# Second product of a mixture-of-experts layer: w2 held in the array and tokens streamed, results turned back a tile later, eight tile sizes in place of six

## The chip, the core and the metric

One core of a Trainium2 chip runs the whole program in one launch. The metric is the time of one execution in microseconds (us). TensorE (PE) multiplies; a matrix product is issued as pairs of a weight load (PEld) of up to 128x128 and a product that streams a second operand past it, one column at a time. VectorE is DVE, ScalarE is ACT, GpSimd is POOL and SyncE, which here only starts transfers, is SP.

## The reference, cut to what matters

2048 tokens of 256 numbers pass a fixed mixing step (each token is rotated by quaternions and scaled by a gate), a router picks one of 8 experts for each, and the expert's gated two-layer network is added to the input:

```
h = x_rot @ w1[e] + b1[e];  a, g = split(h)          # 256 -> 2 x 1024
y = (a * sigmoid(g)) @ w2[e] + b2[e]                  # 1024 -> 256
out = x + y      # e is the expert with the largest router logit of the token
```

All data are float32. With the inputs that are drawn, the experts get 308, 336, 181, 195, 258, 268, 327 and 175 tokens.

## The kernel before, in words

**Early part** (to about 36 us). x is loaded and turned, the rotation matrices are built, the router's logits and the place of every token in its expert's list are worked out on chip, the rotated rows are written to a table in memory (`x_rows`), and a small table (`ctrl`) gets one word per tile with its size class and expert. Near its end PE runs products on zeros (`keep_warm`, `keep_warm_long`).

**Tiles.** There is one tile for each expert, tile 0 to tile 7, of up to 512 tokens in four subtiles of 128; more tiles are taken only if an expert has over 512 tokens, which does not happen here. POOL gathers the rows of a tile by indirect transfers, one for each subtile (`gather`, into `xg`), gathers the rows of x to which the result is added (`fetch`, into `y_out`), and scatters finished rows (`scatter`), always for four subtiles. Its order in tile i is: wait until PE has turned the rows of tile i, gather(i+1), wait for the result of tile i-1, scatter(i-1), fetch(i+1). SP loads the next expert's weights as soon as the raw copies are split.

**Precision.** Every product of two float32 matrices is made of three products of a fast format (fp32r): hi by hi, hi by lo, lo by hi. ACT copies the high part of w1, w2, the tile's rows and u, DVE subtracts it for the low part. All `_hi` and `_lo` names are these.

**First product** (`first_product`, lines 1082 to 1108). w1 is held, the tile's tokens stream. For each of 8 chunks c of hidden units and for g and a, 6 products of n columns follow each other: 96 products for a tile. n is not the number of tokens but the least entry of `SIZES` that holds it; PE has one copy of the body for each size and picks it by comparisons (`by_size`). DVE, ACT and POOL only know the number of subtiles, 2, 3 or 4, and work on 256, 384 or 512 columns (line 602 and line 891 and on). While PE works on chunk c, ACT takes the sigmoid of g (L573), DVE multiplies (L821), ACT and DVE make u_hi (L579) and u_lo (L827).

**Turning the next rows** (`turn_held`, L1057). After the first product of tile i, PE turns the gathered rows of tile i+1, two transposes for each subtile in use.

**Second product** (`second_product`, `row_blocks`, lines 1110 to 1137). Here u is held, 128 tokens at a time, and w2 streams, 256 columns wide: 8 chunks x 3 products for each subtile in use. y comes out with tokens on the partitions, ready to be added to the rows. Subtiles 3 and 2 come first where there are any, then 1, then 0.

**After it.** DVE adds b2, spread over all partitions in `b2_all`, to the fetched rows at chunk 6 of the first product (L836), and adds y to them at chunk 2 of the next tile's first product, in two instructions, one for each bank of y (L850); the scatters of subtiles 0 and 3 go when the first is done, those of 1 and 2 when the second is. For the last tile `add_last` (L858, L863) adds subtile 1 after its products, while those of subtile 0 still run, and each is scattered when it is added (`end_blocks`).

**Code of PE.** `visit` and `landing` are a jump to a place in the later code and back, made in the early part; the landings stand behind the bodies of five of the six sizes.

## Time and profile before

| | |
|---|---|
| median of 3 runs | 214.83 us (214.12 to 215.44) |
| the profiled execution: first to last instruction | 213.9 us |
| the profiled execution's own time as a run | not given beside its span |
| tiles 0 to 7, from the first product of tile 0 to the last of tile 7 | 36.3 to 209.5 us |
| busy: PE, DVE, POOL, ACT | 95%, 74%, 60%, 57% |
| moved by DMA | 41.26 MB, 193 GB/s |

The profile is of one execution. Busy time of PE counts each product from its start until its result is out, so that neighbours overlap: the distance from start to start says how fast the engine works, the duration of one does not. The three runs listed have no span beside them; the 0.9 us between the median and the profiled span is taken as what lies around the span.

### The profile page before, as it was taken

How to read it: one execution, taken by the hardware profiler on the slowest of the kernel's cores; microseconds unless marked ns; L12 is line 12 of the kernel's file. 1: busy time of each engine (PE TensorE's matmuls, PEld its weight loads, DVE VectorE, ACT ScalarE, POOL GpSimd, SP SyncE). 2: the span in 40 equal slices, each digit the busy share in tenths (PEclk: the TensorE clock that was granted, in tenths of full speed). 3: DMA queues.
4: the chain of work that ended last, by engine and by line, in shares of the span. 5: the costliest groups of instructions: out<-in, count | busy, mean ns of one | idle time of the engine just before them, and what ended most of it. 6: DMA issues, size and time to landing. Idle time of an engine off the chain costs nothing.

```text
span 213.9 us, 4367 instructions
## 1 busy us (share of the span) xinstructions
PE 202.7 (95%) x1512; PEld 191.0 (89%) x1513; DVE 158.0 (74%) x308; ACT 122.5 (57%) x206; POOL 129.2 (60%) x163
## 2 busy tenths in 40 slices
PE   7997779999999999999998999999999999999991
PEld 3877625999999999999998999899999999999991
DVE  4918936789928996598888969993998479874950
ACT  2454861576727482667585767564949185735620
POOL 6002467876802888287878877885487817820751
PEclk9999969999999999999999999999999999999998
DMA  5993744889775174937499479738535691820011
GB/s 144 393 365 122 291 142 116 265 300 311 215 193 227 63 259 97 361 90 264 103 296 317 131 219 320 259 76 292 223 135 168 204 287 69 256 44 0 25 40 37
DMA packets 17540, 41.26 MB, mean 193 GB/s; under 512 B 2920, under 2 KB 11241, under 8 KB 15338
## 3 DMA queue, kind: packets, MB, share of 16 engines
q1 hardware_dynamic: 12784, 30.48, 39.9%
q0 software_dynamic: 4512, 10.50, 19.4%
q14 instruction: 19, 0.16, 0.2%
q8 instruction: 7, 0.11, 0.2%
q10 hardware_dynamic: 218, 0.01, 0.1%
HBM read 36.78 MB, written 6.03 MB: 200 GB/s over the span
## 4 chain that ended last, share of the span: by engine, by line
PE 57%; POOL 13%; DVE 12%; issue 7%; DMA 7%; ACT 2%; DVEq 0%; POOLq 0%; ACTq 0%
PE y_ps L1121 7%; DMA xg<-x_rows,g_idx 7%; PE y_ps L1122 6%; PE y_ps L1123 6%; POOL y_out L429 5%; PE g_ps L1101 5%; POOL out_dram L438 5%; PE g_ps L1106 5%; PE g_ps L1102 4%; PE a_ps L1106 4%; PE a_ps L1102 4%; PE a_ps L1101 4%; PE y_ps L931 3%; POOL xg L417 3%; DVE arena L821 3%
## 5 line engine op out<-in xcount | busy, mean ns | idle before, releaser
L438 POOL DMA_INDIRECT out_dram<-y_out,s_idx x30 | 42.1, 1403 | 41.5 <-DVE y_out L850 30.8
L573 ACT ACTIVATE arena<-g_ps,b_t 128x384 f32<-128x384 f32 (+1 forms) x64 | 34.5, 538 | 47.4 <-PE g_ps L1106 47.4
L821 DVE SCALAR_TENSOR_TENSOR arena<-a_ps,b_t,arena 128x384 f32<-128x384 f32 (+1 forms) x64 | 36.1, 564 | 30.5 <-PE a_ps L1106 27.6
L1121 PE MATMUL y_ps<-w_hi,u_hi 128*128 128x256 f32 x168 | 48.6, 289 | 0.1
L429 POOL DMA_INDIRECT y_out<-in_x_dram,g_idx x32 | 42.4, 1325 | 9.8 <-issue 9.8
L1122 PE MATMUL y_ps<-w_lo,u_hi 128*128 128x256 f32 x168 | 47.5, 283 | 0.0
L1123 PE MATMUL y_ps<-w_hi,u_lo 128*128 128x256 f32 x168 | 47.5, 283 | 0.0
L417 POOL DMA_INDIRECT xg<-x_rows,g_idx x32 | 37.2, 1164 | 13.7 <-issue 9.1
L712 DVE TENSOR_TENSOR w_lo<-w_raw,w_hi 128x1024 fp32r<-128x1024 f32 x32 | 37.2, 1220 | 4.8 <-DMA xg<-x_rows,g_idx 3.6
L579 ACT ACTIVATE u_hi<-arena 128x384 fp32r<-128x384 f32 (+1 forms) x64 | 30.7, 479 | 15.5 <-DVE arena L821 15.5
L1101 PE MATMUL g_ps<-xr_hi,w_hi 128*128 128x256 f32 (+3 forms) x128 | 36.9, 301 | 0.3 <-issue 0.2
L1102 PE MATMUL g_ps<-xr_hi,w_lo 128*128 128x256 f32 (+3 forms) x128 | 36.6, 299 | 0.0
L1101 PE MATMUL a_ps<-xr_hi,w_hi 128*128 128x256 f32 (+3 forms) x128 | 36.6, 299 | 0.0
L1102 PE MATMUL a_ps<-xr_hi,w_lo 128*128 128x256 f32 (+3 forms) x128 | 36.6, 299 | 0.0
L1121 PEld LDWEIGHTS y_ps<-w_hi,u_hi 128*128 128x128 f32 x168 | 32.2, 192 | 0.9 <-DVE u_lo L827 0.5
L827 DVE TENSOR_TENSOR u_lo<-arena,u_hi 128x384 fp32r<-128x384 f32 (+1 forms) x64 | 32.0, 500 | 1.1 <-ACT u_hi L579 0.3
L1122 PEld LDWEIGHTS y_ps<-w_lo,u_hi 128*128 128x128 f32 x168 | 32.2, 192 | 0.0
L1123 PEld LDWEIGHTS y_ps<-w_hi,u_lo 128*128 128x128 f32 x168 | 32.2, 192 | 0.0
L526 ACT ACTIVATE w_hi<-w_raw 128x1024 fp32r<-128x1024 f32 x32 | 31.2, 1058 | 0.0
L1106 PE MATMUL g_ps<-xr_lo,w_hi 128*128 128x256 f32 (+3 forms) x128 | 28.1, 300 | 0.0
L1106 PE MATMUL a_ps<-xr_lo,w_hi 128*128 128x256 f32 (+3 forms) x128 | 27.9, 299 | 0.0
L1101 PEld LDWEIGHTS g_ps<-xr_hi,w_hi 128*128 128x128 f32 x128 | 24.2, 189 | 1.0 <-issue 0.8
(167 smaller groups left out, 297.0 us busy)
## 6 DMA issues: line engine op xcount, KB each, us to landing
w_raw<-in_L_ffn_w_dram SPq DMA_DIRECT2D x16, 1024.0 KB, 8.5
w_raw<-in_L_ffn_w_dram SPq DMA_DIRECT2D x16, 512.0 KB, 5.0
arena<-in_x_dram SPq DMA_DIRECT2D x4, 512.0 KB, 5.9
x_rows<-arena SPq DMA_DIRECT2D x8, 256.0 KB, 2.6
b_all<-in_L_ffn_b_dram SPq DMA_DIRECT2D x1, 1024.0 KB, 5.1
xg<-x_rows,g_idx POOLq DMA_INDIRECT x32, 6.1
y_out<-in_x_dram,g_idx POOLq DMA_INDIRECT x32, 4.2
out_dram<-y_out,s_idx POOLq DMA_INDIRECT x30, 4.0
```

The costliest lines, as they stand in the source:

```text
L417: nc.gpsimd.indirect_dma_start(out=xg[:, s * DIM:(s + 1) * DIM], out_offset=None, in_=x_rows, in_offset=bass.IndirectOffsetOnAxis(ap=g_idx ...
L429: nc.gpsimd.indirect_dma_start(out=y_out[i % YB][:, s * DIM:(s + 1) * DIM], out_offset=None, in_=x_flat, in_offset=bass.IndirectOffsetOnAx ...
L438: nc.gpsimd.indirect_dma_start(out=out_flat, out_offset=bass.IndirectOffsetOnAxis(ap=s_idx[:, i * NSUB + s:i * NSUB + s + 1], axis=0), in_ ...
L573: nc.scalar.activation(sig[:, c % SIG_RING, 0:n], pair[c % RING][1][:, 0:n], ACT.Sigmoid, bias=b1_t[:, bass.ds(e * (2 * NC) + (NC + c), 1) ...
L712: V.tensor_tensor(unit_of(w1_lo, u), raw_unit(u), unit_of(w1_hi[:, :].bitcast(F32), u), ALU.subtract)\
L821: V.scalar_tensor_tensor(u32[:, c % (8 - SIG_RING), 0:n], pair[c % RING][0][:, 0:n], b1_t[:, bass.ds(e * (2 * NC) + c, 1)], sig[:, c % SIG ...
L1101: T.matmul(dst, w_part(w1_hi, k), xh, start=(k == 0), stop=False)
L1102: T.matmul(dst, w_part(w1_lo, k), xh, start=False, stop=False)
L1106: last = T.matmul(dst, w_part(w1_hi, k), xr_lo[:, k * ITEM:k * ITEM + n], start=False, stop=(k == KH - 1))
L1121: T.matmul(dst, u_hi[:, uv], w2_hi[:, wv], start=first, stop=False)
L1122: T.matmul(dst, u_hi[:, uv], w2_lo[:, wv], start=False, stop=False)
L1123: last = T.matmul(dst, u_lo[:, uv], w2_hi[:, wv], start=False, stop=final)
```

## The change

The second product holds w2 and streams the tokens. For each half h of the 256 outputs and each chunk c there are 3 products of n columns, where n is the tile's size class; y comes out with the outputs on the partitions (`y_half[h]`). ACT adds b2 there as a bias, one number for each partition, while it copies y to `yt` in SBUF (`biased`, 336 columns whatever the tile; the first half's copy stands between the second and the third part of the next w1 split, the second half's behind the fourth). PE turns `yt` back with six transposes at chunk 2 of the next tile's first product (`turn_back_rows`), into the banks from which it came, and DVE adds the result to the rows in one instruction. A fourth subtile, where a tile has one, is turned ahead of the first product. The last tile is followed by its two copies, eight transposes, and an addition and a scatter for each subtile in use.

`SIZES` goes from six entries to eight, with 224 as the least; the tiles of this input have the classes 320, 336, 224, 224, 272, 272, 336, 224, where they had 320, 352, 256, 256, 288, 288, 352, 256. DVE and ACT work on 256 columns for two subtiles and 336 for three, where it was 384. The load of b2 to all partitions (1 MB) goes; b2 comes as 16 rows early, and is turned on PE with b1. PE has a copy of the second product for each size. Landings stand behind all eight sizes, with three more visits in the early part.

```diff
-    SIZES = (256, 288, 320, 352, 384, 512)
+    SIZES = (224, 256, 272, 288, 304, 320, 336, 512)
     BLOCKS = [(size + P - 1) // P for size in SIZES]
+    WIDTH = {blocks: max(size for size, b in zip(SIZES, BLOCKS) if b == blocks) for blocks in BLOCKS}
+    TURNED = 3
...
-    LANDINGS = (0, 1, 2, 3, 5)
+    LANDINGS = tuple(range(len(SIZES)))
...
+        b_t = sb("b_t", P + KH * NE)
+        b1_t = b_t[:, 0:P]
+        b2_t = b_t[:, P:P + KH * NE]
+        yt = sb("yt", KH * ITEM)
...
-        y_ps = [ps(f"y{h}_ps") for h in range(2)]
+        y_ps = ps("y_ps", KH * 512)
+        y_half = [y_ps[:, h * 512:(h + 1) * 512] for h in range(KH)]
...
@@ -303,6 +309,7 @@
             for g in range(4):
                 sp.dma_start(x_tok[:, 4 * g:4 * g + 4, :], xv[:, 4 * g:4 * g + 4, :]).then_inc(x_loaded[g], 16)
             sp.dma_start(b1_rows[:, :], b1.rearrange("e (c f) -> (e c) f", f=P)).then_inc(b1_loaded, 16)
+            sp.dma_start(b2_rows[:, :], b2.rearrange("e (h f) -> (e h) f", f=P)).then_inc(b2_loaded, 16)
...
             load_w2(0, 1)
-            for s in range(NSUB):
-                sp.wait_ge(gathered[s], 16)
-            sp.dma_start(b2_all[:, :], b2.rearrange("e d -> (e d)").partition_broadcast(P)).then_inc(b2_loaded, 16)
             for e in range(1, NE):
...
+            nc.gpsimd.memset(yt[:, :], 0.0).then_inc(yt_set, 1)
...
             def scatter(i):
-                for s in (0, 3, 1, 2):
-                    if PLACE[s] == 0:
-                        pool.wait_ge(y_done[BANK[s]], i + 2)
+                pool.wait_ge(y_done, i + 2)
+                for s in range(NSUB):
                     scatter_block(i, s)
...
             def end_blocks(blocks):
 
-                pool.wait_ge(last_added, 1)
-                for s in range(1, min(blocks, 3)):
+                for s in range(blocks):
+                    pool.wait_ge(last_added, s + 1)
                     scatter_block(NE - 1, s)
-                pool.wait_ge(last_added, 2)
-                scatter_block(NE - 1, 0)
-                if blocks == NSUB:
-                    pool.wait_ge(last_added, 3)
-                    scatter_block(NE - 1, 3)
...
                 if i > 0:
-                    act.wait_ge(mm2_done, i)
+                    act.wait_ge(half_done[KH - 1], i)
...
             act.wait_ge(b1_turned, 1)
-            nc.scalar.activation(b1_t[:, :], early_ps[:, 0:P], ACT.Copy).then_inc(b1_t_done, 1)
+            nc.scalar.activation(b_t[:, :], early_ps[:, 0:P + KH * NE], ACT.Copy).then_inc(b1_t_done, 1)
...
+            def biased(i, e, h, first, cols, done=None):
+                act.wait_ge(half_done[h], i + 1)
+                put = nc.scalar.activation(yt[:, h * ITEM + first:h * ITEM + cols], y_half[h][:, first:cols], ACT.Identity,
+                                           bias=b2_t[:, bass.ds(e * KH + h, 1)])
+                if done is not None:
+                    put.then_inc(done, 1)
...
                 if 0 < i < NE:
                     for u in range(W1U):
                         w1_hi_part(i, u)
+                        if u % 2 == 1:
+                            biased(i - 1, i - 1, u // 2, 0, FIRST, yt_done[u // 2])
...
+                biased_rest(i, e, n)
+                if i >= NE - 1:
+                    for h in range(KH):
+                        biased(i, e, h, 0, FIRST, yt_done[h])
...
-                if_blocks(act, this_word(act, word_at), lambda blocks: gate_tile(e, e, blocks * P))
+                if_blocks(act, this_word(act, word_at), lambda blocks: gate_tile(e, e, WIDTH[blocks]))
...
+            def add_rows(i):
                 dve.wait_ge(x_fetched[i % YB], (i // YB + 1) * NSUB * 16)
-                rows = y_out[i % YB][:, 0:blocks * DIM].rearrange("p (s d) -> p s d", s=blocks)
-                V.tensor_tensor(rows, rows, b2_all[:, bass.ds(e * DIM, DIM)].unsqueeze(1).to_broadcast([P, blocks, DIM]),
-                                ALU.add).then_inc(b2_added, 1)
...
-            def add_rows(i):
-                dve.wait_ge(mm2_done, i + 1)
-                dve.wait_ge(b2_added, i + 1)
-                for h in range(2):
-                    half = bank_rows(i, h)
-                    V.tensor_tensor(half, y_ps[h][:, :].rearrange("p (s d) -> p s d", s=2), half, ALU.add)\
-                        .then_inc(y_done[h], 1)
+                dve.wait_ge(y_turned, i + 1)
+                rows, y = rows_of(i, 0, NSUB)
+                V.tensor_tensor(rows, y, rows, ALU.add).then_inc(y_done, 1)
...
             def add_last(i, blocks):
 
-                dve.wait_ge(b2_added, i + 1)
-                dve.wait_ge(outer_done, i + 1)
-                rows = bank_rows(i, 1)[:, 0:min(blocks - 1, 2)]
-                V.tensor_tensor(rows, y_ps[1][:, :].rearrange("p (s d) -> p s d", s=2)[:, 0:min(blocks - 1, 2)], rows,
-                                ALU.add).then_inc(last_added, 1)
-                dve.wait_ge(mm2_done, i + 1)
-                for a in range(2 if blocks == NSUB else 1):
-                    rows = bank_rows(i, 0)[:, a]
-                    V.tensor_tensor(rows, y_ps[0][:, a * DIM:(a + 1) * DIM], rows, ALU.add).then_inc(last_added, 1)
-                dve.wait_ge(last_added, 3 if blocks == NSUB else 2)
-                for h in range(2):
-                    dve.sem_inc(y_done[h], 1)
+                dve.wait_ge(x_fetched[i % YB], (i // YB + 1) * NSUB * 16)
+                dve.wait_ge(y_turned, i + 1)
+                for s in range(blocks):
+                    rows, y = rows_of(i, s, 1)
+                    V.tensor_tensor(rows[:, 0], y[:, 0], rows[:, 0], ALU.add).then_inc(last_added, 1)
+                dve.wait_ge(last_added, blocks)
+                dve.sem_inc(y_done, 1)
...
-                n = blocks * P
+                n = WIDTH[blocks]
...
-                    if c == 6:
-                        add_b2(i, e, blocks)
                 lo_u(i, NC - 1, n)
...
                 if f == 3:
                     visit(2)
+                if f == 6:
+                    visit(7)
...
                 rotate_blocks(b)
+                if b == 3:
+                    visit(8)
                 if b == 5:
                     visit(4)
+                if b == 6:
+                    visit(9)
             pe.wait_ge(b1_loaded, 16)
-            T.transpose(early_ps[:, 0:P], b1_rows[:, :], ident[:, :]).then_inc(b1_turned, 1)
+            pe.wait_ge(b2_loaded, 16)
+            T.transpose(early_ps[:, 0:P], b1_rows[:, :], ident[:, :])
+            T.matmul(early_ps[:, P:P + KH * NE], b2_rows[:, :], ident[0:KH * NE, 0:KH * NE], start=True, stop=True)\
+                .then_inc(b1_turned, 1)
 
...
+            def turn_back(subs):
+                for h in range(KH):
+                    for s in subs:
+                        last = T.transpose(y_half[h][:, s * P:(s + 1) * P], yt[:, h * ITEM + s * P:h * ITEM + (s + 1) * P],
+                                           ident[:, :])
+                return last
+            def turn_back_rows(at1, blocks):
+                for h in range(KH):
+                    pe.wait_ge(yt_done[h], at1)
...
+            def first_product(size, i, at1):
                 n = SIZES[size]
                 for c in range(NC):
+                    if c == 2:
+                        with pe.If(((i - 1) & 15) < NE - 1):
+                            turn_back_rows(at1, TURNED)
...
-            def row_blocks(subs, at1, done=None):
-                for c in range(NC):
-                    pe.wait_ge(u_lo_done[c], at1)
-                    wv = slice(c * DIM, (c + 1) * DIM)
-                    for s in subs:
-                        at = c * ITEM + s * P
-                        uv = slice(at, at + P)
-                        dst = y_ps[BANK[s]][:, PLACE[s] * DIM:(PLACE[s] + 1) * DIM]
-                        first = c == 0 and s == subs[0]
-                        final = c == NC - 1 and s == subs[-1]
-                        T.matmul(dst, u_hi[:, uv], w2_hi[:, wv], start=first, stop=False)
-                        T.matmul(dst, u_hi[:, uv], w2_lo[:, wv], start=False, stop=False)
-                        last = T.matmul(dst, u_lo[:, uv], w2_hi[:, wv], start=False, stop=final)
-                if done is not None:
-                    last.then_inc(done, 1)
...
+            def second_product(size, at1):
+                n = SIZES[size]
                 pe.wait_ge(w2_split, at1)
-                for h in range(2):
-                    pe.wait_ge(y_done[h], at1)
-                with pe.If(f_size(word) >= BLOCKS.index(4)):
-                    row_blocks((3,), at1)
-                with pe.If(f_size(word) >= BLOCKS.index(3)):
-                    row_blocks((2,), at1)
-                row_blocks((1,), at1, done=outer_done)
-                row_blocks((0,), at1, done=mm2_done)
+                pe.wait_ge(y_done, at1)
+                for h in range(KH):
+                    dst = y_half[h][:, 0:n]
+                    for c in range(NC):
+                        if h == 0:
+                            pe.wait_ge(u_lo_done[c], at1)
+                        wv = slice(c * DIM + h * P, c * DIM + (h + 1) * P)
+                        uv = slice(c * ITEM, c * ITEM + n)
+                        T.matmul(dst, w2_hi[:, wv], u_hi[:, uv], start=(c == 0), stop=False)
+                        T.matmul(dst, w2_lo[:, wv], u_hi[:, uv], start=False, stop=False)
+                        last = T.matmul(dst, w2_hi[:, wv], u_lo[:, uv], start=False, stop=(c == NC - 1))
+                    last.then_inc(half_done[h], 1)
...
+            def first_and_landing(size, i, at1):
+                first_product(size, i, at1)
+                if size in LANDINGS:
+                    landing(LANDINGS.index(size) + 2)
...
                     at1 = pe.to_reg(i + 1)
+                    next1 = pe.to_reg(i + 2)
                     at16 = pe.to_reg(i * 16 + 16)
                     next16 = pe.to_reg(i * 16 + 32)
...
-                    by_size(word, 0, len(SIZES) - 1, lambda size: first_product(size, at1))
+                    with pe.If(pe.snap(size_before, min_val=0, max_val=len(SIZES) - 1) >= BLOCKS.index(NSUB)):
+                        turn_back_rest(at1)
+                    by_size(word, 0, len(SIZES) - 1, lambda size: first_and_landing(size, i, at1))
+                    pe.reg_mov(size_before, 0)
                     with pe.If(i < NE - 1):
+                        pe.reg_mov(size_before, f_size(word))
                         after = pe.snap(next_word, min_val=0, max_val=127)
                         pe.wait_ge(pair_free[NC - RING], at1)
                         turn_held(after, next16)
-                    second_product(word, at1)
+                    by_size(word, 0, len(SIZES) - 1, lambda size: second_product(size, at1))
+                    with pe.If(i >= NE - 1):
+                        turn_back_rows(next1, NSUB)
+                    pe.nop()
```

## Rows read from the trace of the kernel before

**Rows 1.** The page, busy time, share of the span and instructions; this is PE.

```profile
PE 202.7 (95%) x1512; PEld 191.0 (89%) x1513; DVE 158.0 (74%) x308; ACT 122.5 (57%) x206; POOL 129.2 (60%) x163
```

**Rows 2.** Windows: all tiles, then tiles 2 to 5; length, busy per engine, clock, DMA.

```profile
36.27:209.55 173.28, 172.12 (x1309) 169.83 (x1308) 135.17 (x205) 105.30 (x179) 113.98 (x87) 1.00 0.60 190
84.69:102.88 18.19, 18.19 (x151) 17.78 (x150) 13.86 (x25) 12.50 (x23) 12.11 (x9) 1.00 0.68 225
102.88:122.04 19.16, 18.34 (x153) 18.11 (x152) 16.46 (x28) 12.71 (x23) 15.50 (x13) 1.00 0.75 230
122.04:144.91 22.87, 22.64 (x174) 22.11 (x174) 19.50 (x28) 14.42 (x23) 18.30 (x16) 1.00 0.66 204
144.91:167.56 22.65, 22.54 (x175) 22.02 (x175) 18.32 (x26) 14.42 (x23) 15.62 (x13) 1.00 0.57 198
```

**Rows 3.** Windows: the second products of tiles 1, 4 and 5.

```profile
75.97:84.69 8.72, 8.72 (x75) 8.72 (x74) 7.10 (x10) 4.86 (x7) 7.26 (x5) 1.00 0.54 160
...
135.50:144.91 9.41, 9.23 (x75) 8.92 (x74) 8.39 (x11) 5.60 (x8) 7.58 (x7) 1.00 0.54 169
158.39:167.56 9.17, 9.11 (x76) 8.82 (x74) 8.38 (x11) 5.59 (x8) 7.34 (x7) 1.00 0.59 186
```

**Rows 4.** Timeline of PE, tiles 3 and 4: first and last of 16 such pairs.

```profile
103.36 0.40 PE L1106 MATMUL g_ps<-xr_lo,w_hi 128*128 128x256 f32 x2
...
114.16 0.40 PE L1106 MATMUL a_ps<-xr_lo,w_hi 128*128 128x256 f32 x2
...
122.56 0.42 PE L1106 MATMUL g_ps<-xr_lo,w_hi 128*128 128x288 f32 x2
...
134.41 0.43 PE L1106 MATMUL a_ps<-xr_lo,w_hi 128*128 128x288 f32 x2
```

**Rows 5.** Chain of waits, tile 6, n = 352: first and last of 16 such pairs.

```profile
168.44 0.32 PE g_ps L1106 x2
...
182.83 0.32 PE a_ps L1106 x2
```

**Rows 6.** Timeline of PE, early part: plain float32 products, 128 columns (`rotate_blocks`).

```profile
19.54 1.06 PE L1002 MATMUL g_ps<-b_all,x_t 128*128 128x128 f32 x8
...
22.22 1.06 PE L1002 MATMUL a_ps<-b_all,x_t 128*128 128x128 f32 x8
```

**Rows 7.** Chain of waits, the turning before tile 4: a gather, one transpose.

```profile
108.46 6.65 DMA xg<-x_rows,g_idx
...
115.59 0.11 PE a_ps L1057
```

**Rows 8.** Waits of PE for tile 4's rows: total, times, longest us.

```profile
PE a_ps L1057 <- DMA xg<-x_rows,g_idx: 0.6, 1, 0.6
```

**Rows 9.** Timeline of DVE and POOL in tile 2: both additions, first scatter.

```profile
89.97 1.28 DVE L850 TENSOR_TENSOR y_out<-y_ps,y_out 128x512 f32<-128x512 f32 x2
...
90.93 1.02 POOL L438 DMA_INDIRECT out_dram<-y_out,s_idx  x1 [3.88 <-DVE y_out L850]
```

**Rows 10.** Timeline of the end: last product, last addition, last scatter.

```profile
209.30 0.28 PE L1123 MATMUL y_ps<-w_hi,u_lo 128*128 128x256 f32 x1
209.61 0.42 DVE L863 TENSOR_TENSOR y_out<-y_ps,y_out 128x256 f32<-128x256 f32 x1 [2.38 <-PE y_ps L1123]
210.31 0.98 POOL L438 DMA_INDIRECT out_dram<-y_out,s_idx  x1 [1.82 <-DVE y_out L863]
```

**Rows 11.** The page, costliest groups: ACT's sigmoids and the idle time before them.

```profile
L573 ACT ACTIVATE arena<-g_ps,b_t 128x384 f32<-128x384 f32 (+1 forms) x64 | 34.5, 538 | 47.4 <-PE g_ps L1106 47.4
```

**Rows 12.** Waits, all engines: POOL in the early part.

```profile
POOL over L398 <- DVE sm L749: 15.4, 1, 15.4
```

**Rows 13.** Timeline of DVE, tile 1: the addition of b2, between products.

```profile
75.21 0.95 DVE L836 TENSOR_TENSOR y_out<-y_out,b_all 128x768 f32<-128x768 f32 x1
```

**Rows 14.** Chain of waits, just ahead of the loop over the tiles.

```profile
31.14 1.07 issue
```

**Rows 15.** The page, DMA queues: packets, MB, share of 16 engines.

```profile
q8 instruction: 7, 0.11, 0.2%
```

More of the change, by code:

```diff
@@ L118, in early @@
             taken[0] += cols
-            return b2_all[0:rows, taken[0] - cols:taken[0]]
+            return scratch[0:rows, taken[0] - cols:taken[0]]
         q_rows = sb("q_rows", QD, rows=13)
         b1_rows = early(P, P)
+        b2_rows = early(KH * NE, P)
         sgn_l = early(P, 64)
@@ L244, in adaln_moe_ffn_kernel @@
         u_lo_done = [sem(f"u_lo_done{c}") for c in range(NC)]
-        mm2_done = sem("mm2_done")
-        outer_done = sem("outer_done")
+        half_done = [sem(f"half_done{h}") for h in range(KH)]
+        yt_set = sem("yt_set")
+        yt_done = [sem(f"yt_done{h}") for h in range(KH)]
+        y_turned = sem("y_turned")
         last_added = sem("last_added")
-        y_done = [sem(f"y_done{h}") for h in range(2)]
+        y_done = sem("y_done")
         scattered = [sem(f"scattered{b}") for b in range(YB)]
@@ L580, in hi_u, with biased_rest @@
                     .then_inc(u_hi_done, 1)
+            FIRST = WIDTH[NSUB - 1]
+            def biased(i, e, h, first, cols, done=None):
[4 more added lines that the diff above has]
+                    put.then_inc(done, 1)
+            def biased_rest(i, e, n):
+                if n > FIRST:
+                    for h in range(KH):
+                        biased(i, e, h, FIRST, n)
             def gate_tile(i, e, n):
@@ L828, in lo_u, with rows_of @@
                                 u_hi[:, at:at + n].bitcast(F32), ALU.subtract).then_inc(u_lo_done[c], 1)
-            def add_b2(i, e, blocks):
-                if i == 0:
-                    dve.wait_ge(b2_loaded, 16)
+            def rows_of(i, first, count):
+                return (y_out[i % YB][:, first * DIM:(first + count) * DIM].rearrange("p (s h d) -> p s h d", s=count, h=KH),
+                        y_ps[:, :].rearrange("p (h s d) -> p s h d", h=KH, s=NSUB)[:, first:first + count])
@@ L1080, in turn_first, with turn_back_rest @@
                         keep_warm(late_ps, 3)
-            def first_product(size, at1):
+            def turn_back(subs):
[5 more added lines that the diff above has]
+            def turn_back_rows(at1, blocks):
+                for h in range(KH):
+                    pe.wait_ge(yt_done[h], at1)
+                turn_back(range(blocks)).then_inc(y_turned, 1)
+            def turn_back_rest(at1):
+                for h in range(KH):
+                    pe.wait_ge(yt_done[h], at1)
+                turn_back(range(TURNED, NSUB))
+            def first_product(size, i, at1):
                 n = SIZES[size]
                 for c in range(NC):
+                    if c == 2:
+                        with pe.If(((i - 1) & 15) < NE - 1):
+                            turn_back_rows(at1, TURNED)
                     if c % CPU1 == 0:
@@ L1142, in by_size @@
                     body(low)
-                    if low in LANDINGS:
-                        landing(LANDINGS.index(low) + 2)
                     return
```

24 lines of the change are left out of this document (10 added, 14 removed).

## The prediction

> **What bounds the kernel now.** I read the busy times first: PE is busy for 95% of the span, nobody else above 74% [rows 1]. That alone would also be true of an engine that waits often and briefly, so the next view is the timeline, where only distances between starts count. In tile 3, at n = 256, there are 90 products from the first start shown to the last, in 10.80 us: 0.1200 us each. In tile 4, n = 288, it is 11.85/90 = 0.1317 [rows 4]; in tile 6, n = 352, 14.39/90 = 0.1599 [rows 5]. These are dense, and the cost follows the columns. The windows then give what is not dense: tile 3 takes 19.16 us where tile 2, of the same size, takes 18.19 [rows 2], partly for two more transposes and 0.6 us because PE waits for the gathered rows of tile 4 [rows 8]; and a second product of 72 streams, which should take 72 x 0.12 = 8.64 us and takes 8.72 in tile 1, takes 9.41 and 9.17 in tiles 4 and 5 [rows 3], where DVE is late with u_lo. So PE bounds all eight tiles, POOL's gathers touch the path once, and 173.28 us [rows 2] is the part that can move. The granted clock is 1.00 in it, the 2.4 GHz level.
>
> **The second product.** Before, 24 products of 256 columns for each subtile in use, 504 in all. After, 48 products of n columns for each tile, 384 in all. n = 272 lies halfway between two rows: 0.1258. For 320 and 336 I go along the line from 288 to 352, 0.00044 us a column: 0.1458 and 0.1529 [rows 4, 5].
> - Tile 0: 8.64 - 48 x 0.1458 = 1.64 us less.
> - Tiles 1 and 6: 8.64 - 48 x 0.1529 = 1.30 less each.
> - Tiles 4 and 5: 9.41 and 9.17 [rows 3] against 48 x 0.1258 = 6.04: 3.37 and 3.13 less. This counts the late u_lo as gone: DVE loses the addition of b2, 0.95 us at the very end of the first product [rows 13], and works on 336 columns where it had 384, and the first pass now takes 3 x 0.126 = 0.38 us for a chunk where it took 0.36, so each u_lo is asked for a little later. Next late would be the sigmoids behind the w2 split on ACT.
>
> **The narrow tiles.** Tiles 2, 3 and 7 go to 224 columns, in 96 + 48 products each. No row shows the fast format below 256. The lines through 256 give 0.1067 (from 352) or 0.1083 (from 288); not a bit faster than now would be 0.1200; a plain float32 product streams 128 columns each 2.68/24 = 0.1117 with the same size of weight load [rows 6], so that a weight load can follow at least that fast. I take 0.110, near that row: 144 x 0.010 = 1.44 us less in each tile, 4.32 in all.
>
> **The first products of the others.** 352 to 336 saves 96 x 0.0070 = 0.67 in tiles 1 and 6, 288 to 272 saves 96 x 0.0059 = 0.57 in tiles 4 and 5, tile 0 keeps 320.
>
> With the 0.6 us wait taken out for now, less work on PE is 1.64 + 2.60 + 6.50 + 4.32 + 1.34 + 1.14 + 0.60 = 18.1 us. Here a page can be weighed against the rows. The Trainium skill, "TensorE: Matmul & The Clock Gate", section "Back-to-back issue gap", puts a warm product at its columns over 2.4 plus 2.5 ns, 0.109 us for 256; the row has 0.1200. By it the second product would fall from 504 x 0.109 = 55.0 to 45.1 us, 9.9 less, where my terms for dense streams give 10.9: the rows make each product that goes dearer, and I go by them.
>
> **Added on PE.** Six transposes in each of tiles 1 to 7, 0.11 us each [rows 7]: 4.62 us, all on the path. PE waits there for ACT's copy of y; ACT starts it as the second product ends, and PE has two chunks (24 products, 2.6 us at least) before it asks, so nothing is late. Left: 18.1 - 4.6 = 13.5 us.
>
> **Moved past other queues.** ACT gets two copies, about 0.54 us each, the mean of its sigmoids [rows 11]; it sat idle 47.4 us in all waiting for PE's g, so they are free; the third and fourth w1 splits wait for the first half of y, about 3 us into the second product, when the first two splits are hardly over, and chunk 4 needs them some 6 us later. If that cover went, ACT's 2 x 0.54 a tile would reach PE's first chunk. Behind the copy of the second half stands the first sigmoid of the tile, whose g comes 0.7 us after. On POOL the memset of `yt` lies within the 15.4 us in which it waits for the counts [rows 12]. On SP one more small load stands ahead of the first weights, and 1 MB of broadcast b2 goes; neither is waited for. The added transpose of b2 and three visits of the early part I cost at nothing, between -0.1 (less DMA) and +1.07 us, the one gap there in which PE waits for nothing shown [rows 14].
>
> **What is late next: the gathers.** POOL's scatter of tile 1 starts 6.24 us after tile 2's first product (90.93 and 84.69 [rows 9, 2]). Now y is added after 0.66 us of transposes, 36 products come 0.36 earlier, and no scatter leaves before both halves are added, half of 1.28 us later [rows 9]: 7.2 us after. Tile 2 starts 1.64 + 1.97 - 0.66 = 2.95 us earlier, at 81.7; the scatter at 88.9. From there POOL has no break until the third gather of tile 4, 17.5 us later (108.46 - 90.93), at 106.4, and this lands 6.65 us after, at 113.1 [rows 7, 9]. PE, which was ready for it at 114.5, is ready 2.95 + (1.44 - 0.66) + (0.96 - 0.66) = 4.0 us earlier, at 110.5. It waits 2.6 us. The same reckoning for tile 5 leaves nothing. Left: 10.9 us.
>
> **The end.** From the start of the last product to the end it is 213.9 - 209.3 = 4.6 us, of which the last 3.6 begin with the last scatter [rows 10]; subtile 1 had gone before. After: 0.31 until y can be read, 0.54 ACT's copy, 0.15 handed on (an estimate, half of the 0.28 from DVE to POOL), 7 x 0.11 to the last transpose's start, 0.31, addition 0.42, 0.28, first scatter and gap 1.28, then 3.6: 7.7 us. 3.1 more, bounds 2 and 4. Net 10.9 - 3.1 = 7.8 us: the span goes from 213.9 to 206.1, and with the 0.9 by which the median of 214.83 stands above the span, **207.0 us**.
>
> **Rivals.**
> - POOL's chain stretches: the 6.65 us of a landing grow, or the scatters run at the slow pace that they have beside DVE's work, and the later tiles wait as well. For: POOL works without a break there, and a shorter tile gives it no less to do. Against: tiles 6 and 7 have slack. The same 2.3 us once more gives 209.3. Chance 0.12.
> - PE's code. It has eight copies of the first product for six, and eight of the second for none. The page shows 7 fetches of instructions on one queue, 0.11 MB [rows 15], and a gap of 1.07 us where the loop's first code is entered [rows 14]. If each of 14 entries (8 second products, and 6 first products of another size than the one before, the first counted) cost 1.07 us, it is 15 us: 222; hidden by a third, half or more, 207 to 217. It decides at 7.8/14 = 0.56 us an entry. Against: PE's stream shows no gap at any tile's start now. Chance 0.15. The Trainium skill, "Runtime: NRT & Kernel Launch", section "Instruction fetch mechanics", speaks for this rival: PE's instruction memory is 128 KiB, filled in 16 KiB blocks, and a branch out of what is held waits for a fetch; no row shows the limit.
> - Slower, by one mechanism: below 256 columns the fast format falls to the plain one's rate. Plain float32 takes two of the shown records for a product (four products in the code stand as x8 [rows 6]), 0.223 us for 128 columns, so 0.39 for 224. 432 narrow products x 0.28 = 121 us: 328. It decides as soon as a narrow product takes 7.8/432 = 0.018 us more than I say, at 0.128. For: nothing in this trace streams it narrower. Against: the cost from 352 to 256 is straight. Chance 0.08.
> - That the size classes do not fit can be excluded: the counts of tokens fix them, and the old classes follow from the same counts.
>
> **Numbers.** The forecast has 0.60, the rivals 0.12, 0.15 and 0.08, and 0.05 is left for what I have not seen. Low end: no wait for gathers (-2.6) and 224 at 0.1067 (-1.4), 203. High end: 224 at 0.1200 (+4.3, of which 0.9 lies in the wait), the gathers' rival (+2.3) give 212.7, and a third of the code's 15 us gives 212; 213.5. What stays out is most of the last rival and the worse half of the code's. A measurement here tells about 1% from no change, so faster is below 212.7 and slower above 217.0. Faster: 0.59 + 0.11 + 0.07 + 0.02 = 0.79. Within: 0.09. Slower: 0.12, 0.08 of it the narrow products.
>
> **What would show it.** L1101 to L1106 at 224 columns about 0.11 us apart, and the second product's 48 streams of tile 4 in some 6.1 us without a gap; one wait of 2 to 3 us of PE's turning ahead of tile 4 and none after; six transposes at chunk 2 that wait for nothing; 7 to 8 us from the last product to the end, with ACT's copy, the eight transposes and two scatters in a row. I am wrong if PE shows gaps at the starts of second products that no engine released (code), if narrow products are over 0.12 apart, or if the tiles 5 to 7 wait for gathers.

## The result: 424.1 us in place of 214.8

The changed kernel takes 424.1 us (median of 4 runs, 419.98 to 440.47, the highest of them in a slower state of the chip), 1.965 times the time of before (95% interval 1.9504 to 1.9795). The forecast of 207.0 us, range 203.0 to 213.5, is wrong by a factor of two, and no rival's time reached it either (the highest was 328).

### The profile page after: what moved, and what is told of

Its sections match the earlier page's. It is cut to its first block, busy times and chain, and to the rows that moved or that the text cites. A ratio compares the mean times of both kernels' runs of the same rounds, so it can differ in the third digit from the quotient of the medians.

```text
span 423.3 us, 4317 instructions
## 1 busy us (share of the span) xinstructions
PE 235.5 (56%) x1444; PEld 218.1 (52%) x1445; DVE 148.0 (35%) x293; ACT 127.8 (30%) x222; POOL 120.7 (29%) x166
## 3 DMA queue, kind: packets, MB, share of 16 engines
q8 instruction: 99, 1.62, 1.9%
## 4 chain that ended last, share of the span: by engine, by line
PE 55%; issue 42%; ACT 1%; DVE 1%; POOL 0%; DVEq 0%
PE y_ps L1158 6%; PE y_ps L1159 5%; PE g_ps L1137 5%; PE y_ps L1160 5%; PE a_ps L1138 5%; PE g_ps L1138 5%; PE g_ps L1142 4%; PE a_ps L1137 4%; PE a_ps L1142 4%; PE y_ps L935 2%; PE y_ps L1099 2%; PE a_ps L1008 1%; PE y_ps L930 1%; PE g_ps L1008 1%; PE a_ps L1070 1%
## 5 line engine op out<-in xcount | busy, mean ns | idle before, releaser
L1137 PE MATMUL g_ps<-xr_hi,w_hi 128*128 128x224 f32 (+3 forms) x128 | 41.2, 335 | 106.6 <-issue 106.6
L844 DVE SCALAR_TENSOR_TENSOR arena<-a_ps,b_t,arena 128x336 f32<-128x336 f32 (+1 forms) x64 | 34.1, 533 | 157.4 <-PE a_ps L1142 154.1
L1137 PEld LDWEIGHTS g_ps<-xr_hi,w_hi 128*128 128x128 f32 x128 | 27.8, 217 | 108.5 <-issue 108.5
L574 ACT ACTIVATE arena<-g_ps,b_t 128x336 f32<-128x336 f32 (+1 forms) x64 | 32.9, 513 | 158.9 <-PE g_ps L1142 158.8
L1158 PE MATMUL y_ps<-u_hi,w_hi 128*128 128x224 f32 (+3 forms) x128 | 45.8, 358 | 40.2 <-issue 40.2
L1158 PEld LDWEIGHTS y_ps<-u_hi,w_hi 128*128 128x128 f32 x128 | 31.5, 246 | 41.5 <-issue 41.5
L1159 PE MATMUL y_ps<-u_hi,w_lo 128*128 128x224 f32 (+3 forms) x128 | 44.6, 348 | 0.0
L1160 PE MATMUL y_ps<-u_lo,w_hi 128*128 128x224 f32 (+3 forms) x128 | 44.2, 346 | 0.0
L1138 PE MATMUL a_ps<-xr_hi,w_lo 128*128 128x224 f32 (+3 forms) x128 | 39.3, 320 | 2.5 <-issue 2.5
L1138 PE MATMUL g_ps<-xr_hi,w_lo 128*128 128x224 f32 (+3 forms) x128 | 39.6, 322 | 0.0
L1137 PE MATMUL a_ps<-xr_hi,w_hi 128*128 128x224 f32 (+3 forms) x128 | 39.2, 319 | 0.0
```

The costliest lines, as they stand in the source:

```text
L574: nc.scalar.activation(sig[:, c % SIG_RING, 0:n], pair[c % RING][1][:, 0:n], ACT.Sigmoid, bias=b1_t[:, bass.ds(e * (2 * NC) + (NC + c), 1) ...
L844: V.scalar_tensor_tensor(u32[:, c % (8 - SIG_RING), 0:n], pair[c % RING][0][:, 0:n], b1_t[:, bass.ds(e * (2 * NC) + c, 1)], sig[:, c % SIG ...
L1137: T.matmul(dst, w_part(w1_hi, k), xh, start=(k == 0), stop=False)
L1138: T.matmul(dst, w_part(w1_lo, k), xh, start=False, stop=False)
L1158: T.matmul(dst, w2_hi[:, wv], u_hi[:, uv], start=(c == 0), stop=False)
L1159: T.matmul(dst, w2_lo[:, wv], u_hi[:, uv], start=False, stop=False)
```

## The profile after

Lines of the page: busy time; the span in 40 slices for PE and for its granted clock, in tenths; the queue that brings instructions (fetches, MB, share); the chain that ended last, by engine.

```profile
PE 235.5 (56%) x1444; PEld 218.1 (52%) x1445; DVE 148.0 (35%) x293; ACT 127.8 (30%) x222; POOL 120.7 (29%) x166
PE   7475499450692548524943086703944039383952
PEclk9588589785696959675978569665978559866887
q8 instruction: 99, 1.62, 1.9%
PE 55%; issue 42%; ACT 1%; DVE 1%; POOL 0%; DVEq 0%
```

PE was busy for 95% of the span and is busy for 56%, with fewer instructions [rows 1]. No other engine is busy for more than 35%, so none bounds the kernel instead. Read the second line: dense slices stand beside empty ones. The fourth line of the block is to be set beside [rows 15]: 99 fetches of instructions for 7, of 16.4 KB each (1.62 MB over 99). In the fifth "issue", time in which PE waits for nothing that the profile shows, is 42% of the chain.

What PE waits for (total, times, longest, us):

```profile
PE g_ps L1137 <- issue: 106.6, 8, 23.3
PE y_ps L1158 <- issue: 40.2, 9, 8.0
PE a_ps L1070 <- issue: 9.0, 4, 2.5
PE a_ps L1008 <- issue: 4.8, 2, 3.1
PE g_ps L1008 <- issue: 4.1, 1, 4.1
PE a_ps L971 <- issue: 3.8, 1, 3.8
PE g_ps L971 <- issue: 3.2, 1, 3.2
PE a_ps L1138 <- issue: 2.5, 2, 1.3
PE y_ps L1099 <- issue: 1.6, 1, 1.6
PE y_ps L1018 <- issue: 1.6, 1, 1.6
```

L1137 is the first product's first line, and the eight times are the eight tiles; L1158 is the same for the second product; L1070 turns the next rows. These stand where PE enters a body or leaves one; L1138 and L1099 lie within a first product, and their gaps are short. L1008, L971 and L1018 lie in the early part, where the visits go out and back: tile 0 starts at 60.28 us, where it started at 36.27 [rows 2].

The chain of waits around the first product of tile 1 (start us, us, what):

```profile
90.96 18.12 issue
109.08 0.62 PE g_ps L1137
109.70 0.28 PE g_ps L1138
109.98 0.28 PE g_ps L1137
...
114.31 0.15 PE a_ps L1137
114.46 0.15 PE a_ps L1138
...
115.23 0.66 PE y_ps L1099 x6
...
127.37 7.65 issue
```

18 us of nothing, then products of 336 columns 0.28 us apart, and from 114.3 on 0.15 apart: the array comes out of the gap at the lower clock level (1.2 GHz) and is back at the upper one (2.4 GHz) at 114.3. Within the gap of 18.12 us the queue of instructions shows 5 fetches. The windows of three whole tiles (0, 2 and 5) say the same in their granted clock, 1.00 before (each line: the window, its length, busy time of five engines, clock, DMA share, GB/s):

```profile
60.28:109.08 48.80, 24.88 (x150) 24.30 (x151) 17.89 (x26) 15.00 (x25) 16.65 (x14) 0.77 0.51 152
154.06:196.74 42.68, 21.91 (x154) 21.33 (x155) 15.08 (x24) 13.58 (x25) 14.40 (x12) 0.74 0.36 110
291.42:345.98 54.56, 24.76 (x156) 23.82 (x157) 16.59 (x24) 14.77 (x25) 13.58 (x12) 0.69 0.28 86
```

Tile 2, 42.7 us where it was 18.2 [rows 2], has its PE busy for 21.9: half of the tile is gap.

## The experiments

**Theories.** *Code*: PE holds a limited amount of its program; the loop over the tiles jumps within a stretch that no longer fits, so that at each entry of a body the instructions are fetched anew. *Jumps*: the new tests and branches on PE are slow by themselves, whatever the amount of code. *Mechanism of the product*: w2 held, or 224 columns, is slow. *Visits*: the three more trips of the early part.

Sizes of code are counts of PE's instructions, branches included, in which a product counts as two, a weight load and a stream, and each wait as one: 2173 before, 3429 after. A fetch moves 16,384 bytes and the Trainium skill gives 256 instructions to such a block ("Runtime: NRT & Kernel Launch", section "Instruction fetch mechanics"). By that count the loop of before lies in 8 blocks and that of after in 13. No run shows that a wait takes a place of its own. The expectations of e1 to e4 count without the waits: 1765 and 2886, so that the two whole programs would be 6.9 and 11.3 blocks long in place of 8.5 and 13.4. All numbers of blocks below go by the count with the waits and are estimates; the kernels that have both counts come in the same order by length in either.

**e1_dead2, e2_dead1: code that never runs.** The kernel before, with size classes that no tile takes:

```diff
-    SIZES = (256, 288, 320, 352, 384, 512)
+    SIZES = (256, 288, 320, 352, 384, 416, 448, 512)   # e1_dead2
+    SIZES = (256, 288, 320, 352, 384, 416, 512)        # e2_dead1
...
```

> The kernel before with two more size classes (416 and 448) that no expert's count reaches: PE has two more bodies of the first product that never run, 2153 PE instructions in the code where the kernel before has 1765 and the changed one 2886. All work is the same. Theory C (PE's code no longer stays in its memory, and branches wait for fetches): well above 250 us, with over 40 instruction fetches on the queue that had 7, and PE gaps released by nobody ahead of first products. Theory W (the change's own work costs the time: the form of the second product, narrow streams, transposes and their waits): 214.8 us, no change within 1%.

> As the last, with one class never used (416): 1959 PE instructions. Theory C: between 214.8 us, if this still fits, and some 250 us, if it does not; it brackets where the step is. Theory W: 214.8 us.

Measured: 251.7 us (1.171, 1.1597 to 1.1829) for 2607 instructions, and 252.5 and 256.7 in the two runs with 2390, which is 9 blocks for the loop; both fetch 28 times. One body that never runs, 217 instructions, costs at least 37 us (252.5 against 215.1 of before, run beside it), and a second one adds nothing that these runs can tell. Of e1_dead2 more was expected, well above 250 us and over 40 fetches. From the timeline of PE in e2_dead1, five of its gaps (in brackets the idle time before and its end):

```profile
57.65 0.32 PE L1057 MATMUL a_ps<-ident,xg 128*128 128x128 f32 x1 [1.89 <-issue]
90.56 0.28 PE L1122 MATMUL y_ps<-w_lo,u_hi 128*128 128x256 f32 x1 [1.94 <-issue]
108.68 0.55 PE L1101 MATMUL g_ps<-xr_hi,w_hi 128*128 128x256 f32 x1 [9.39 <-issue]
147.55 0.29 PE L1101 MATMUL g_ps<-xr_hi,w_hi 128*128 128x288 f32 x1 [0.23 <-issue]
227.30 0.55 PE L1101 MATMUL g_ps<-xr_hi,w_hi 128*128 128x256 f32 x1 [5.48 <-issue]
```

Between 108.68 and 193.49 four tiles with the two smallest sizes run with no gap over 0.7 us and 3 fetches; the long gaps are at the tiles that go to another end of the code, 352 to 256 the worst. That is what *Code* says and no other theory.

**e9_pad_behind: the same amount, out of the loop.** 223 instructions that never run, behind the loop (2396 in all, more than e2_dead1 has):

```diff
+            with pe.If(last_tile >= TAB - 1):
+                keep_warm(late_ps, 110)
```

> The kernel before with 220 PE instructions that never run, placed behind the loop over the tiles: the program is 2396 PE instructions long, as with one unused size class (2390, 254.6 us), but the loop's own stretch of code is that of the kernel before. If the program's whole length decides: 240 to 260 us. If only the stretch that the loop jumps about in decides: 214.8 us within 1%, and 7 or 8 fetches.

Measured: 216.1 us, 1.0024 (0.9979 to 1.0068), 8 fetches. So code behind the loop is free; what counts is the stretch within which the loop jumps. Between the 8 blocks of before and the 9 of e2_dead1 lies an edge. Its number of blocks hangs on the count; that it lies between these two kernels does not.

**e4_second_alone, e5_sizes_alone: each part of the change.** The new second product with the six old sizes (2731 instructions), and the eight sizes with their landings and visits under the old second product (2619):

```diff
-    SIZES = (224, 256, 272, 288, 304, 320, 336, 512)
+    SIZES = (256, 288, 320, 352, 384, 512)
-    LANDINGS = tuple(range(len(SIZES)))
+    LANDINGS = (0, 1, 2, 3, 5)
...
```

> The changed kernel with the six old size classes (256 to 384, 512) and the old landings: w2 held, y turned back, b2 added by ScalarE; 2268 PE instructions. Theory C: 250 to 400 us, as the other kernels that do not fit. Theory W: 400 us or more if the new second product is to blame, about 215 us if it is the eight sizes.

> The kernel before with the change's eight size classes and its three more visits, and nothing of the new second product (u is held, w2 streams 256 columns). The code of PE is as long as in the kernel with two unused classes (2619 PE instructions by the compiled program's count, waits and branches too, where the kernel before has 2173). Theory C (fetches of code): slower than before, 230 to 300 us, over 25 fetches. Theory W: 205 to 215 us, since there are only fewer columns to stream.

Measured: 292.8 us (1.362, 1.3535 to 1.3713; 39 fetches) and 289.8 (1.348, 1.3393 to 1.356; 43). Each half alone goes out of bounds by about the same code and costs about the same; together, 209 us, they cost more than the sum of 78 and 75. That this is because the loop spreads further is in keeping with the 99 fetches, for 39 and 43, and is argued.

**e6_old_visits.** The changed kernel without its three added visits:

```diff
-    LANDINGS = tuple(range(len(SIZES)))
+    LANDINGS = (0, 1, 2, 3, 4)
-                if f == 6:
-                    visit(7)
...
```

> The changed kernel without its three added visits, with landings behind the first five classes. It tells whether the visits are what makes the early part 24 us longer (tile 0 started at 60.3 us in the changed kernel and at 36.3 before). If each visit to code that isn't held costs a fetch, the early part is 8 to 12 us shorter than with them, and the loop stays as slow: 405 to 420 us. If the visits serve the loop, it is slower than 424 us.

Measured: 407.4 us (1.894, 1.8789 to 1.9096), 90 fetches; tile 0 starts at 47.19, 13 us earlier. The three visits and their landings, costed at nothing, are worth 17 us; the rest stays.

**e3_four_sizes, e7_four_landed: the change in code that fits.** The changed kernel with four classes, 2041 instructions. Tile 0 takes 336 in place of 320, the other tiles keep their columns. In e7_four_landed the landings stand ahead of the bodies, and a sixth landing, behind them, and its visit, which e3_four_sizes has not, are there (2045):

```diff
-    SIZES = (224, 256, 272, 288, 304, 320, 336, 512)
+    SIZES = (224, 272, 336, 512)
...
             def first_and_landing(size, i, at1):
+                landing(LANDINGS.index(size) + 2)              # e7_four_landed
                 first_product(size, i, at1)
-                if size in LANDINGS:                           # e7_four_landed
-                    landing(LANDINGS.index(size) + 2)
...
+                    landing(6)                                 # e7_four_landed
```

> The changed kernel with four size classes, 224, 272, 336 and 512, and without the visits of the landings that go: 1654 PE instructions, fewer than before. Every tile streams what it streams in the changed kernel, but tile 0, which goes from 320 to 336 (+1.0 us). Theory C: no fetches in the loop, and the time that was forecast for the change plus 1.0: 208 us (204 to 214). Theory W: 400 us or more, since the work is that of the changed kernel.

> The kernel with four classes again (2045 PE instructions), but with the landings ahead of the bodies instead of behind, so that the five visits go through its code in steps of less than 16 KB as in the kernel before. In the run with four classes the tiles began 9.2 us later than before, with two gaps of 3.5 and 2.4 us that nothing released, at visits. If these are fetches that a nearer landing starts in time: tile 0 begins at 36 to 38 us, and the time is some 9 us under the 222.9 us of that run, 211 to 215 us. If the delay has another cause, 220 to 224 us.

Measured: 222.9 us (1.040, 1.032 to 1.048; 10 fetches), then 214.05 (0.997, 0.9941 to 0.9999; 7). e3_four_sizes still loses 3.5 and 2.4 us where visits come back (L971, L1016), at a lower clock behind them, and starts tile 0 at 45.49. With the landings at the front and the sixth one it starts at 35.10; the two were not tried apart. The expectation of e3_four_sizes, 204 to 214 us, failed by this early part and by the branches of the last experiment below; that of e7_four_landed held. PE and the code queue of e7_four_landed, from its page:

```profile
PE 191.7 (91%) x1444; PEld 180.2 (86%) x1445; DVE 146.1 (69%) x293; ACT 125.4 (60%) x222; POOL 123.5 (59%) x162
q8 instruction: 7, 0.11, 0.2%
```

and the largest wait of its PE within the tiles:

```profile
PE g_ps L1131 <- issue: 5.6, 8, 1.1
```

The same number of products and transposes as in the changed kernel, 1444, and 210 us below it. The difference can be added up for the two profiled executions: the span is 213.0 us shorter (423.3 - 210.3). The waits "issue" of the changed kernel sum to 159.9 in the tiles and 17.5 in the early part; of such, 7.4 are left in e7_four_landed (5.6, and 1.5 and 0.3 elsewhere), so 170.0 is waiting for code. PE's busy time falls from 235.5 to 191.7: 43.8, which is what the lower clock cost after the gaps. 213.8 in all, within 1 us of what is to be explained. That answers *Mechanism of the product*.

**e8_four_merged.** 5.6 us were left ahead of the first products, 0.2 to 1.1 for each tile, and from 60 us on with no fetch. Is it the comparisons that choose a body? Here one choice in each tile leads to first product, turning and second product in a row:

```diff
-                    by_size(word, 0, len(SIZES) - 1, lambda size: second_product(size, at1))
...
+                with pe.If(i < NE - 1):                        # within the body of a size
...
+                    turn_held(after, pe.to_reg(i * 16 + 32))
+                second_product(size, at1)
```

> As the last, with first product, turning and second product of a class in one body, so that PE chooses the body once a tile and not twice (2141 PE instructions). In the run with four classes PE stood 0.8 to 1.0 us between the second product of a tile and the next first product, behind narrow tiles above all, with nothing released there. If that is the time of PE's branches, they shrink to 0.3 us or less and this is 3 to 5 us under the kernel with the landings moved alone, 207 to 211 us. If the gaps come from waits on other engines, the two are equal.

Measured: 214.0 us (0.9944, 0.9914 to 0.9975), where 207 to 211 was expected if it is; 5.3 us in 7 gaps of 0.2 to 1.4. The second choice of a tile is not it. The first one, just ahead of the gaps, is still there, and e12_four_lean answers for it.

**e10_before_four, e11_before_five: the fair kernel before.** The old second product with the sizes of e7_four_landed, and with 320 added, landings ahead of the bodies:

```diff
-    SIZES = (256, 288, 320, 352, 384, 512)
+    SIZES = (224, 272, 336, 512)                           # e10_before_four
+    SIZES = (224, 272, 320, 336, 512)                      # e11_before_five
```

> The kernel before with the four classes 224, 272, 336, 512 and landings ahead of the bodies, the old second product: narrower first products alone, in code that fits (1739 PE instructions). Per tile, 96 x 0.009 us less at 224, 96 x 0.006 at 272, 96 x 0.007 at 336 instead of 352, 0.7 more in tile 0: 4.4 us less on PE, some of it lost where POOL's gathers end: 210 to 213 us. Its distance to the kernel with four classes and the new second product (214.05 us) is what the new second product is worth once its code fits: if that one was a gain as I forecast, this is slower than 214; if it pays back in transposes, gaps and the end what it saves, this is faster.

> As the last, with 320 kept as a fifth class (1956 PE instructions): tile 0 streams what it did, 0.7 us less than with four. 209.5 to 212.5 us; the best that these experiments point to.

Measured: 214.4 us (0.995, 0.9909 to 0.9991; 1739 instructions, 6 fetches) and 223.6 (1.039, 1.0314 to 1.0473; 1956, 10), where 210 to 213 and 209.5 to 212.5 were expected. The first gives back part of what its shorter tiles save: tile 0 starts at 37.64, 1.4 us later than before, and PE waits 1.0 us for gathers in two places. The second fits by its length, and from 60 us on it fetches nothing, but it is 9 us slower all the same; its waits:

```profile
PE a_ps L1057 <- issue: 3.7, 2, 3.1
PE y_ps L931 <- issue: 2.5, 1, 2.5
PE a_ps L1057 <- DMA xg<-x_rows,g_idx: 1.8, 2, 0.9
```

The gap of 3.1 us stands behind the first product of tile 0. What is seen is 4 fetches more than e10_before_four has, and a first tile of 29.2 us; that some blocks had not been visited when tile 0 began is argued and was not tried.

**e12_four_lean: three branches away.** e7_four_landed without three branches in each tile: the condition around the turning at chunk 2 (in tile 0 it turns zeros), the register and test for a fourth subtile, and the test for the last tile, whose turning moved behind the loop. It leaves out the fourth subtile of y and the spare tiles, which do not occur with these counts.

```diff
-                        with pe.If(((i - 1) & 15) < NE - 1):
-                            turn_back_rows(at1, TURNED)
+                        turn_back_rows(at1, TURNED)
...
-                    with pe.If(pe.snap(size_before, min_val=0, max_val=len(SIZES) - 1) >= BLOCKS.index(NSUB)):
-                        turn_back_rest(at1)
...
-                    with pe.If(i >= NE - 1):
-                        turn_back_rows(next1, NSUB)
-                    pe.nop()
+            turn_back_rows(pe.to_reg(NE + 1), NSUB)
```

> The kernel with four classes and the landings ahead, with three branches of PE taken out of each tile: the test at chunk 2 (tile 0 turns a block of zeros in its place), the turning of a fourth subtile of the tile before, and the test for the last tile, whose transposes stand behind the loop. It leaves out tiles of four subtiles and spare tiles, which this input does not have. If the gaps of 0.3 to 1.1 us ahead of each first product (5.6 us in all) are the time of PE's branches, they shrink by a half or more: 210.5 to 212.5 us. If they are anything else, they stay, and the time is 214 us.

Measured: **208.4 us**, 0.968 (0.9596 to 0.9764), 2020 instructions, 7 fetches: faster than both kernels, and faster than its expectation. PE is busy for 93% of its span of 205.8 us. What PE waits for ahead of the first products and of the turnings:

```profile
PE g_ps L1130 <- issue: 0.9, 3, 0.4
PE a_ps L1064 <- DMA xg<-x_rows,g_idx: 0.5, 1, 0.5
```

5.6 us of waits ahead of the first products became 0.9, with the choice of the body still in place, and the spans differ by 4.5 (210.3 and 205.8; the medians by 5.7). *Jumps* was a true theory of small size: the three branches, with the register and the empty instruction (`nop`) that went with them, cost some 0.6 us in a tile there, 5 us in all, against some 210 for the code. Which of them costs what was not tried.

## Why the prediction was wrong, point by point

**The step that failed** is the pricing of PE's code, in the rival of that name and in "three visits I cost at nothing". The rival named the place (entries of bodies that no engine releases) and the sign, and the Trainium skill's section spoke for it. But it took the 1.07 us of [rows 14] as the price of one of 14 entries and got 15 us at most. The waits are 106.6/8 = 13.3 us at a first product and 40.2/9 = 4.5 at a second, and a long one holds several fetches (5 in the 18.12 us ahead of tile 1): 99 fetches, 177.4 us of waits. And the clock's 43.8 us were in no term. The sign that the prediction gave for this rival, gaps at the starts of second products that no engine released, is there, but the larger part stands at the first products. The argument "PE's stream shows no gap at any tile's start now", used against the rival, was the wrong way round: the kernel before stood less than one body of 217 instructions below the edge (e2_dead1), and rows from below an edge say nothing of the far side. What was at hand and not used: the number of PE's instructions, which the diff raises by 8 copies of 48 products and two of 96, less the 96 of the old second product. The 0.15 for this rival was too little, and its price of 15 us, a wait for each entry and nothing more, was no upper bound.

By the Trainium skill ("Runtime: NRT & Kernel Launch", section "Instruction fetch mechanics"), PE's memory for instructions is 128 KiB, 8 blocks. By the count with the waits the runs agree: 8 blocks of loop run with 7 fetches in 215 us, 9 with 28 in 252.5 and 256.7; without the waits the edge would lie lower, so the size itself is not shown here. The same section calls the memory a FIFO in which only sequential prefetch helps; in the kernel before, a loop that jumps backwards seven times fetches nothing from 54 us on. On that the measurement decides.

The prediction also set a formula of the Trainium skill beside its rows ("TensorE: Matmul & The Clock Gate", section "Back-to-back issue gap"). That section gives it for an isolated product, not for a stream of weight loads and products; the rows by which the prediction went were the better guide (0.1117 us measured below at 224 columns, 0.096 by the formula, an estimate).

**The sum itself**, which the changed kernel cannot show, can be read in e12_four_lean, which differs from the change by its classes, landings and branches. Its tile 0 has 336 columns, 144 x 0.0071 = 1.0 us more, so the forecast for it is a span of 207.1 and a median of 208.0 us; measured 205.8 and 208.4.

**Narrow tiles, 0.110 us a product: right.** The timeline of PE, 18 products at 224 columns in tile 2:

```profile
90.43 0.28 PE L1130 MATMUL g_ps<-xr_hi,w_hi 128*128 128x224 f32 x1
...
92.44 0.27 PE L1130 MATMUL a_ps<-xr_hi,w_hi 128*128 128x224 f32 x1
```

2.01/18 = 0.1117 us, the distance of [rows 6] and 0.0017 over the value taken: 0.7 us in 432 products. The rival of the plain rate is out.

**Second product of tile 4 in 6.04 us, u_lo no longer late: right.** The window of it:

```profile
132.24:138.55 6.31, 6.26 (x52) 6.07 (x50) 5.81 (x9) 5.77 (x10) 5.09 (x5) 1.00 0.66 209
```

6.31 us, with some 0.2 of them between its last product and the next tile, where it was 9.41 [rows 3]. Its last product starts 5.97 us after its first: 5.97/47 = 0.127.

**Six transposes in 0.66 us a tile, waiting for nothing: right.** The chain of waits has them as one piece in each tile but tile 3, where it runs over POOL and a gather; the one of tile 2:

```profile
84.58 0.66 PE y_ps L1093 x6
```

**Gathers 2.6 us late before tile 4: too much**, 0.5 us, and no other wait for gathers is shown. That rival is out too.

**The end, 7.7 us: nearly right.** The last product starts at 198.61 and the span ends at 205.8, 7.2 us. The timeline of all engines:

```profile
198.92 0.54 ACT L588 ACTIVATE yt<-y_ps,b_t 128x336 f32<-128x336 f32 x1 [2.14 <-PE y_ps L1153]
199.64 1.06 PE L1093 MATMUL y_ps<-ident,yt 128*128 128x128 f32 x8 [0.76 <-ACT yt L588]
200.81 0.76 DVE L871 TENSOR_TENSOR y_out<-y_ps,y_out 128x256 f32<-128x256 f32 x2 [5.51 <-PE y_ps L1093]
201.51 0.98 POOL L443 DMA_INDIRECT out_dram<-y_out,s_idx  x1 [6.57 <-DVE y_out L871]
```

Copy, eight transposes, addition and scatter follow each other as the prediction has them.

**Added tests and branches, not costed: wrong by about 5 us**, which this kernel had to take out first. Then the span misses the forecast by -1.3 us: gathers -2.1, tile 0 at 34.78 for 36.27 -1.5, the end -0.5, against +0.7 for narrow products and +1.2 for waits "issue" that are left (0.9 and a 0.3 ahead of a turning); 0.9 stays without a name. That the median comes within 0.4 us is partly luck: it stands 2.6 above the span, where the forecast took 0.9. Each run listed stands some 1.7 us above its own span (207.55 and 205.8 here), so that the profiled execution of before took about 215.6 by its span (an estimate), above its median of 214.83, while that of e12_four_lean lies below its own. The 0.9 of the forecast was not the time around a span.

With the branches in, the change is worth nothing even where its code fits: 214.05 us against 214.40 of the old second product with the same sizes (e7_four_landed, e10_before_four). The 208.4 us of e12_four_lean are not quite like for like with these, since it leaves out what they can do with a fourth subtile; the old second product was not tried with its own tests taken out.

## What to carry to other kernels

Before adding a copy of a body, or a size class, to a loop, count the engine's instructions from the first to the last address that the loop jumps between, dead bodies too: the cost is a cliff (217 instructions that never run cost at least 37 us here), and a trace from below it shows nothing. In the profile the signs are the fetches of the instruction queue and waits "issue" at the entries of bodies, with the clock falling behind each. To learn what such a change is worth in itself, run it with fewer classes, and take the branches off the engine that bounds.

## What the runs showed of the hardware

- PE's loop of before (8 blocks by the count with waits) fetches nothing from 54 us on; with one body more that never runs (9) it is 37 us slower at least (e2_dead1). In the changed kernel (13) the stretch from tile 0 to the end is 363.0 us, for 175.2 in e7_four_landed. Code behind the loop is free (e9_pad_behind).
- After gaps of 3.3 to 23.3 us PE ran on at the lower level, 0.28 us for 336 columns where 0.15 is the full pace: 43.8 us of busy time in this kernel.
- The landings matter: 222.9 us with them behind the bodies (e3_four_sizes), 214.05 with them ahead and a sixth one (e7_four_landed), for the same computation.
- Tests and branches on PE are not free between dense products: about 5 us for three in each of 8 tiles (e7_four_landed and e12_four_lean), and nothing is fetched there from 60 us on.
